# Cross attention with each quadrant's own maximum, a third projection bank and the first results moved

## The reference

```
q = x @ Wq + bq                  # 64 x 512, 16 heads of 32, scaled by 32**-0.5
k = ctx @ Wk + bk                # 1601 x 512
v = ctx @ Wv + bv                # 1601 x 512
s = q_h @ k_h.T, masked where the key is not valid      # 64 x 1601 for each head h
p = softmax(s)                   # over the 1601 keys
o = p @ v_h
```

## Time and profile before

| | us |
|---|---|
| median of three runs | 2890.74 (2889.43 to 2891.78) |
| the profiled execution, time | 2892.8 |
| the profiled execution, span from first to last instruction | 2891.1 |
| PE busy | 2660.4 |
| DVE busy | 1671.3 |
| ACT busy | 1441.8 |
| cross attention stage, about | 847 to 2318 |

### The profile page before, as it was taken

One profiled execution on the slowest core, in us unless ns is written; L12 is line 12 of the kernel. 1 busy time (PEld: TensorE's weight loads), 2 busy tenths in 40 slices (PEclk: granted clock), 3 DMA queues, 4 the chain that ended last, 5 costly groups with the idle time before them and its releaser, 6 DMA issues. The chain is left out here.

```text
span 2891.1 us, 58626 instructions
## 1 busy us (share of the span) xinstructions
PE 2660.4 (92%) x24696; PEld 2075.1 (72%) x24696; DVE 1671.3 (58%) x3485; ACT 1441.8 (50%) x2943; POOL 114.1 (4%) x104
## 2 busy tenths in 40 slices
PE   6999899899869999999999999999999987789987
PEld 3444677789757887778777877778777765667764
DVE  4333542557565555665655556655556678864487
ACT  2112222336435566565665656656666622725775
POOL 0000200120010000000000000000000013010000
PEclk9999999999979999999999999999999988899988
DMA  7998102347751011111111111111111020114300
GB/s 257 311 311 282 48 4 66 125 147 268 235 171 30 20 48 49 47 26 26 49 48 47 26 26 49 48 41 31 26 49 39 31 63 1 40 44 161 117 16 30
DMA packets 202932, 249.40 MB, mean 86 GB/s; under 512 B 77728, under 2 KB 132000, under 8 KB 202416
## 3 DMA queue, kind: packets, MB, share of 16 engines
q1 hardware_dynamic: 193456, 220.49, 24.2%
q10 hardware_dynamic: 6656, 16.78, 1.8%
q0 software_dynamic: 2560, 8.39, 0.8%
HBM read 221.50 MB, written 24.12 MB: 85 GB/s over the span
## 5 line engine op out<-in xcount | busy, mean ns | idle before, releaser
L91 PE MATMUL xa_J<-xa_c_hi,xa_wk_hi 128*128 128x402 f32 x1024 | 369.9, 361 | 1.7 <-POOL xa_m L2491 1.7
L2380 DVE TENSOR_TENSOR cl_v<-xa_J,main_x 128x512 f32<-128x512 f32 (+1 forms) x208 | 143.5, 690 | 390.2 <-PE xa_J L93 301.5
L93 PE MATMUL xa_J<-xa_c_hi,xa_wk_lo 128*128 128x402 f32 x1024 | 354.7, 346 | 0.0
L92 PE MATMUL xa_J<-xa_c_lo,xa_wk_hi 128*128 128x402 f32 x1024 | 354.5, 346 | 0.0
L2245 ACT ACTIVATE xa_kT<-xa_J,cl_bk 128x402 f32<-128x402 f32 x256 | 151.5, 592 | 383.7 <-PE xa_J L93 380.5
L91 PE MATMUL xa_J<-xa_wv_hi,xa_c_hi 128*128 128x512 f32 (+1 forms) x832 | 339.0, 407 | 0.4 <-ACT xa_kT L2245 0.4
L93 PE MATMUL xa_J<-xa_wv_hi,xa_c_lo 128*128 128x512 f32 (+1 forms) x832 | 327.7, 394 | 0.0
L92 PE MATMUL xa_J<-xa_wv_lo,xa_c_hi 128*128 128x512 f32 (+1 forms) x832 | 327.2, 393 | 0.0
L2258 ACT ACTIVATE xa_pr<-xa_pr,xa_nm 128x416 f32<-128x416 f32 x512 | 321.5, 631 | 3.9 <-DVE xa_nm L2364 3.9
L2264 ACT ACTIVATE xa_pr<-xa_pr,xa_ri 128x416 f32<-128x416 f32 x512 | 280.1, 630 | 60.4 <-DVE xa_ri L2368 60.1
L2354 DVE CUSTOM_DVE_ANT_0 xa_pr<-xa_S,xa_m 128x416 f32<-128x416 f32 x512 | 271.8, 587 | 43.6 <-PE xa_S L2536 29.3
(11 more groups left out here) (516 smaller groups left out, 4962.2 us busy)
## 6 DMA issues: line engine op xcount, KB each, us to landing
bl_rows<-in_ctx SPq DMA_DIRECT2D x40, 1024.0 KB, 8.8
main_x<-in_ctx_cols SPq DMA_DIRECT2D x192, 201.0 KB, 2.6
bl_cols<-in_ctx_cols SPq DMA_DIRECT2D x24, 1024.0 KB, 10.5
moe_raw<-in_L_ffn_routed_w SPq DMA_DIRECT2D x45, 512.0 KB, 4.8
main_qoT<-in_L_ffn_w ACTq DMA_DIRECT2D x32, 512.0 KB, 4.0
main_x<-in_ctx_cols SPq DMA_DIRECT2D x64, 197.5 KB, 3.3
main_qoT<-in_L_attn_W SPq DMA_DIRECT2D x16, 512.0 KB, 3.7
routed_in<-main_qoT SPq DMA_DIRECT2D x1, 7680.0 KB, 22.6
```

The source lines that it names most:

```text
L91: pe.matmul(out, w_hi, x_hi, start=first, stop=False)
L92: pe.matmul(out, w_hi, x_lo, start=False, stop=False)
L93: return pe.matmul(out, w_lo, x_hi, start=False, stop=last)
L2380: nc.vector.tensor_tensor(v[0:rows(n), value_slot(b, n), :], J[0:rows(n), place(b, ("v", n)) % 2, :], bv_sb[0:rows(n), :], ALU.add)\
```

## The change

Exponentials are taken with each partition's own maximum (that of its quadrant of the keys). `negate` turns the maxima into biases right behind the masks. When the exponentials are done, `weigh` copies biases and sums of the four quadrants beside each other on 32 partitions (four copies), takes the smallest bias and the differences to it; ACT takes their exponentials (`shares`); `invert` weighs the sums with the shares, adds them up, inverts, and writes share times inverse back to the four quadrants (four instructions) as `ri`, by which `normalise` scales as before.

PE loses `send_max`, `spread_max` and `sums`. The bank `E` goes to `J`, which now has three banks. `result(w)` at the end of a batch is moved behind the first key tile of the next batch, and the result after it behind the second key tile. ACT's copies of the key tiles and its exponentials are interleaved anew, and some of DVE's `turn`, `lows` and `keep_values` change places.

```diff
+BANKS = 3
...
+        local = s.sb("local", [P, 2, 2 * HG])
+        nm, rs = local[:, 0, :], local[:, 1, :]
+        parts = s.sb("parts", [QB, 4, 2, 2 * HG])
+        apart, share, weighed = (s.sb(n, [QB, 4, 2 * HG]) for n in ("apart", "share", "weighed"))
+        least, whole, inverse = (s.sb(n, [QB, 2 * HG]) for n in ("least", "whole", "inverse"))
...
-        J = s.ps("J", [P, 2, 512])
-        O, E = s.ps("O", [P, 512]), s.ps("E", [P, 512])
-        X, Y, Z = E[0:2 * HG, 0:P], E[:, P:P + 2 * HG], E[:, P + 2 * HG:P + 4 * HG]
+        J = s.ps("J", [P, BANKS, 512])
+        O = s.ps("O", [P, 512])
...
+                def shares(w):
+                    act.wait_ge(apart_ready, w + 1)
+                    nc.scalar.activation(share[:], apart[:], ACT.Exp).then_inc(share_ready, 1)
+
                 def normalise(w):
-                    act.wait_ge(inv_ready, w + 1)
+                    act.wait_ge(inv_ready, 4 * (w + 1))
...
                 def probabilities(w):
-                    exps(w - 1, 0, 4)
+                    keep_key(w, 0)
+                    exps(w - 1, 0, 3)
+                    keep_key(w, 1)
+                    exps(w - 1, 3, 6)
                     keep_key(w, 2)
-                    exps(w - 1, 4, 6)
+                    exps(w - 1, 6, 8)
                     keep_key(w, 3)
-                    exps(w - 1, 6, 8)
+                    shares(w - 1)
...
                 for b in range(BATCH):
                     w = GR * b
                     if b:
+                        keep_key(w, 0)
+                        exps(w - 1, 0, 2)
+                        keep_result(w - 4)
                         highs(b, 3, 0, 2)
-                        keep_result(w - 4)
-                        keep_key(w, 0)
+                        keep_key(w, 1)
                         highs(b, 3, 2, 4)
                         keep_result(w - 3)
-                        keep_key(w, 1)
-                        probabilities(w)
-                        keep_result(w - 2)
+                        exps(w - 1, 2, 5)
+                        keep_key(w, 2)
+                        exps(w - 1, 5, 8)
+                        keep_key(w, 3)
+                        shares(w - 1)
                         widen_mask(b)
                         normalise(w - 1)
-
-                    keep_key(w + 1, 0)
-                    keep_key(w + 1, 1)
+                        keep_result(w - 2)
+
                     probabilities(w + 1)
+                    normalise(w)
                     if b:
                         keep_result(w - 1)
-                    normalise(w)
-
-                    keep_key(w + 2, 0)
-                    keep_key(w + 2, 1)
+
                     probabilities(w + 2)
...
+                    if b == LAST:
+                        probabilities(w + 3)
+                        normalise(w + 2)
+                    else:
+                        keep_key(w + 3, 0)
+                        exps(w + 2, 0, 3)
+                        keep_key(w + 3, 1)
+                        exps(w + 2, 3, 6)
                         highs(b + 1, 0)
+                        keep_key(w + 3, 2)
+                        exps(w + 2, 6, 8)
+                        keep_key(w + 3, 3)
+                        shares(w + 2)
                         highs(b + 1, 1)
-                    probabilities(w + 3)
-                    normalise(w + 2)
-                    if b < LAST:
+                        normalise(w + 2)
                         highs(b + 1, 2)
...
-                def largest(w):
-                    dve.wait_ge(max_out, w + 1)
-                    nc.vector.tensor_reduce(gmax[:], X.rearrange("i (c q) -> i q c", c=4)[:, None, :, :].to_broadcast([2 * HG, 4, QB, 4]),
-                                            AX.X, ALU.max, negate=True).then_inc(gmax_ready, 1)
-
-                def keep_largest(w):
-                    dve.wait_ge(max_back, w + 1)
-                    nc.vector.tensor_copy(nm[:], Y).then_inc(nm_ready, 1)
-
-                def inverse(w):
-                    dve.wait_ge(summed, w + 1)
-                    nc.vector.reciprocal(ri[:], Z).then_inc(inv_ready, 1)
+                def negate(w):
+                    dve.wait_ge(masked, 2 * HG * (w + 1))
+                    nc.vector.tensor_scalar(nm, mx[:], -1.0, None, ALU.mult).then_inc(nm_ready, 1)
+
+                def weigh(w):
+                    dve.wait_ge(exp_done, 2 * HG * (w + 1))
+                    for c in range(4):
+                        nc.vector.tensor_copy(parts[:, c, :, :], local[QB * c:QB * (c + 1), :, :]).then_inc(gathered, 1)
+                    dve.wait_ge(gathered, 4 * (w + 1))
+                    nc.vector.tensor_reduce(least[:], parts[:, :, 0, :].rearrange("q c i -> q i c"), AX.X, ALU.min).then_inc(least_ready, 1)
+                    dve.wait_ge(least_ready, w + 1)
+                    nc.vector.tensor_tensor(apart[:], least[:, None, :].to_broadcast([QB, 4, 2 * HG]), parts[:, :, 0, :], ALU.subtract)\
+                        .then_inc(apart_ready, 1)
+
+                def invert(w):
+                    dve.wait_ge(share_ready, w + 1)
+                    nc.vector.tensor_tensor(weighed[:], share[:], parts[:, :, 1, :], ALU.mult).then_inc(weighed_ready, 1)
+                    dve.wait_ge(weighed_ready, w + 1)
+                    nc.vector.tensor_reduce(whole[:], weighed[:].rearrange("q c i -> q i c"), AX.X, ALU.add).then_inc(whole_ready, 1)
+                    dve.wait_ge(whole_ready, w + 1)
+                    nc.vector.reciprocal(inverse[:], whole[:]).then_inc(inverse_ready, 1)
+                    dve.wait_ge(inverse_ready, w + 1)
+                    for c in range(4):
+                        nc.vector.tensor_tensor(ri[QB * c:QB * (c + 1), :], share[:, c, :], inverse[:], ALU.mult).then_inc(inv_ready, 1)
...
                     if b:
-                        turn(w - 2, 0, 2)
-                        largest(w - 1)
-                        lows(b, 3, 0, 2)
-                        keep_largest(w - 1)
-                        lows(b, 3, 2, 4)
-                        turn(w - 2, 2, 8)
+                        turn(w - 2, 0, 3)
+                        lows(b, 3)
+                        turn(w - 2, 3, 8)
+                        weigh(w - 1)
                         keep_values(b, 0)
-                        inverse(w - 1)
+                        invert(w - 1)
                         masks(w, 0)
                         keep_values(b, 1)
                         masks(w, 1)
-
-                    largest(w)
+                        negate(w)
+
                     if b:
-                        turn(w - 1, 0, 2)
-                    keep_largest(w)
-                    if b:
-                        turn(w - 1, 2, 8)
+                        turn(w - 1, 0, 8)
+                        weigh(w)
+                        invert(w)
                         keep_values(b, 2)
                     else:
+                        weigh(w)
                         keep_values(b, 3)
-                    inverse(w)
+                        invert(w)
                     masks(w + 1, 0)
                     keep_values(b, 3 if b else 4)
                     masks(w + 1, 1)
+                    negate(w + 1)
                     if b and not last:
                         keep_values(b, 4)
...
+                    turn(w, 0, 8)
+                    weigh(w + 1)
                     keep_values(b, 4 if last else 5)
-                    inverse(w + 1)
+                    invert(w + 1)
...
                     else:
-                        turn(w + 1, 2, 5)
+                        turn(w + 1, 0, 8)
+                        keep_values(b, 9)
                         lows(b + 1, 0)
-                        keep_largest(w + 2)
-                        keep_values(b, 9)
-                        turn(w + 1, 5, 8)
+                        weigh(w + 2)
+                        keep_values(b, 10)
+                        invert(w + 2)
+                        masks(w + 3, 0)
                         lows(b + 1, 1)
-                        keep_values(b, 10)
-                        inverse(w + 2)
-                        masks(w + 3, 0)
                         keep_values(b, 11)
-                        lows(b + 1, 2, 0, 2)
                         masks(w + 3, 1)
+                        negate(w + 3)
                         keep_values(b, 12)
-                        lows(b + 1, 2, 2, 4)
+                        lows(b + 1, 2)
...
                 w = QUADS - 1
-                turn(w - 1, 0, 2)
-                largest(w)
+                turn(w - 1, 0, 4)
                 keep_values(LAST, 8)
-                turn(w - 1, 2, 4)
-                keep_largest(w)
+                turn(w - 1, 4, 8)
                 keep_values(LAST, 9)
-                turn(w - 1, 4, 8)
-                keep_values(LAST, 10)
                 for k in range(KC):
                     low_out(k)
+                weigh(w)
+                keep_values(LAST, 10)
```

(46 more changed lines are left out.)

34 lines of the change are left out of this document (10 added, 24 removed).

## The result

| | before | changed |
|---|---|---|
| median, us | 2890.09 (2888.26 to 2891.78) | 2838.07 (2836.60 to 2838.65) |
| profiled execution, us | 2892.8 | 2838.65 |
| its span, us | 2891.1 | 2836.9 |
| first key matmul of the stage to the first matmul of the next stage, us | 1474.81 | 1419.53 |
| of that: batch 0 | 86.13 | 83.97 |

Four executions of each kernel stand beside one another; the ratio is 0.9819, with a 95% interval of 0.9802 to 0.9836. The gain is 52 us by the medians and 54 by the profiled executions, where 68 was forecast: 2838.07 against 2822.7, and 1 us outside of the range. The stage gave 55.3, of which the 15 full batches gave 53.8 against 65.6 forecast, batch 0 gave 2.2 against 1.8, and the tail lost 0.7 where it was to gain 0.6. What lies behind the stage takes 569.1 us before and 568.4 after.

What follows compares the result with a forecast made beforehand. PE was taken to bound the stage: 4.37 us a batch over 15 batches (65.6), 1.8 in batch 0 and 0.6 in the tail made 68 us, so a median of 2822.7 us, with an 8 in 10 range of 2815 to 2837.

Steps and rivals of the forecast that it cites:

- batch 0: The first batch, without a first quad or results: three quads at 0.60 us each, a gain of 1.8 us.
- the tail: The end of the stage: one set of small matmuls goes, a gain of 0.6 us.
- What bounds the kernel: PE ends the cross attention stage; work taken off it gains its whole distance, work added to DVE or ACT is free.
- The moved result: At a batch's end: PE's trip over DVE's copy of value tile 12 goes, gaining 1.75 us a batch, and 0.1 more.
- The small matmuls: On PE: removing the two transposes and their pauses gains 0.49 us per quad without results; removing sums gains 0.11 or 0.32.
- The third bank: PE's projection banks: the added bank gains nothing by itself, only covering later copies on ACT and DVE.
- The length of `invert`: On DVE ahead of the masks: 0.9 us if four operations overlap, 1.4 if all seven are chained; 1.2 taken.
- the due time of the fourth mask: In a tight quad, needed 4.6 us after the first scores start, so `invert` may last 1.65 us without cost.
- rival B: `invert` takes 2.0 us, costing 0.35 in each of 33 tight quads, 12 us: 2834 us; chance 0.12.
- A: Pauses around PE's small matmuls belong to waits and banks and stay; only 55 us gained, 2836 us; chance 0.09.
- C: DVE's small operations cost 0.68 us each like the replaced reduction, `invert` 4.8: 2949 us, slower by 58; chance 0.03.
- D: Batch 0's exponentials start earlier and an early PE pause goes, 2 to 5 us more, 2819 us; chance 0.15.

Runs made afterwards that it cites:

- e1: The changed kernel with `invert` ahead of the value copy in the five places where it stood behind one; 2827.78 us, ratio to before 0.9779.
- e7: The changed kernel without the exchange between quadrants, each partition normalised by its own sum; 2822.04 us, ratio to before 0.9762.
- e4: The changed kernel with the first result of a batch back at the batch's end; 2865.63 us, ratio to before 0.9911.
- e5: The kernel before with only its first two results moved behind the next batch's first and second key tiles, ACT's copies with them; 2864.79 us.
- e6: The changed kernel with two banks and, in 48 quads, two transposes of constants where the old ones stood; 2862.22 us, ratio to before 0.9898.
- e3: The changed kernel with two projection banks instead of three; 2838.93 us, ratio to before 0.9820.
- e2: The changed kernel with the reciprocal in `invert` taken twice, the second waiting for the first; 2846.85 us, ratio to before 0.9851.
- e2b: e1 with the reciprocal in `invert` taken three times in a chain; 2831.12 us, ratio to before 0.9787.
- e10: The changed kernel run once more, unaltered; 2836.82 us, ratio to before 0.9810.
- e8: e1 with, in the tail, the copy of value tile 12 ahead of the turns and `weigh` and `invert` ahead of the low parts; 2831.46 us.
- e9: e8 with value tile 3 put between the first two halves of the scores in batch 0; 2824.26 us, ratio to before 0.9766.
- e11: e9 with DVE's low parts ahead of `weigh` again in the tail; 2824.47 us, ratio to before 0.9758.

## Why the prediction was wrong in size

**What bounds the kernel: right.** PE did. Removing its waits and small matmuls gave nearly their whole distance, and 768 more instructions on DVE gave nothing away in the full batches where they lay beside PE's work (e1 against e7).

**The moved result: right.** 1.85 a batch forecast, 1.63 (e4) and 1.83 (e5) measured. No wait for `c_lo` or for `turned` took its place.

**The small matmuls: right.** 8.91 us for four key tiles (8.9 forecast); e6 shows that 0.45 for a pair of transposes, where 0.49 was forecast, is the price of the matmuls themselves. The third bank was given nothing and is worth nothing (e3).

**The length of `invert`: right, at the upper end.** 0.9 to 1.4 was given, 1.2 taken, 1.41 measured. The three chained steps start 0.20 to 0.23 after one another, and the four products take 0.72 for four, 0.18 each and not the 0.08 of an overlapped one. By the Trainium skill, VectorE: DVE Perf Modes, section "Two Vector instructions with no wait between them", they had to, since they write to four quadrants; the trace agrees. Taking the rule's 1.4 would by itself not have changed the sum, since the step below allowed 1.65. With the due time right it would have counted: by the estimate of 1.06, an `invert` of 1.2 costs (1.2 - 1.06) x 33 = 4.6 us and one of 1.41 the 11.5 measured.

**The failed step: the due time of the fourth mask.** The prediction says "its fourth head, three quarters of 0.9 later, needs the fourth mask at t + 4.6. In hundredths, I may be 1.65 us." I had divided the half's 0.91 us equally among its four heads, as if they ran one after another. They don't. All 32 weight loads of a half pass in 0.23 us, the four heads run beside one another, and the 0.91 is common to them. Taken one by one, the 32 matmuls of a free half start in two groups of 16, at 1413.66 to 1413.76 and at 1414.03 to 1414.13, so the fourth head's first matmul starts within 0.1 us of the first head's. Worked back from the measured loss, the fourth mask is due at about t + 4.0 and `invert` may last about 1.06. It lasted 0.35 more, in 33 quads: 11.5 us, 10.4 of them in the 15 batches. That is the size and the wait of rival B (0.35 in 33 quads, 12 us, 2834), which I gave 0.12; it came by another road, for `invert` was not 2.0 long but the margin was 0.6 shorter. e1 takes the 10.3 us out, e2 adds 0.23 to each as such a due time demands, and e2b shows twice that addition nearly free elsewhere (0.5 us in the 15 batches).

**The rest.** Without that term (e1) the 15 batches give 64.2 us where 65.6 was forecast. The transposes are 1.9 of what is missing (20.2 by e6 for 22.1). That batch 0 gave 2.2 (1.8 in e10) for the 1.8 forecast is partly luck: three late masks, about 1.0, are in it, and its stretch at the 1.2 GHz level differs between executions. Without the late masks (e1) it is 2.8. The tail was put at +0.6 and came at -0.7 (-0.35 in e10). The forecast counted only its small matmuls there; I had not followed DVE's list in the tail, where the copy of value tile 12 now stands behind four turns that wait for ACT's later scaling, so that PE waits 2.0 us for it and not 0.8. e8 removes that wait.

**Rivals.** A falls by e6, B's place is shown with another cause, C falls by the 0.20 us reductions. D, the early pause of PE, did not come by itself; it is there to be had (e9).

## What to carry to other kernels

When a chain is moved off the bound engine, its length matters less than where it stands: the same seven instructions cost 10 us between a copy and the masks and nothing ahead of the copy. Read due times from the first use, here the weight loads, and never from an equal share of a group's duration, since packed matmuls start together. Follow the moved order through the first batch and the tail as well; they hold their own waits. Here they gave 7 us more of the stage (e1 to e11), though the medians' ratios, 0.9779 and 0.9758, hardly tell the two apart.

## What the runs showed of the hardware

- Four heads packed in the array as 32 x 32 tiles load all 32 weights in 0.23 us and are done after 0.91 us together; a fourth head whose weights are 0.22 us late makes the whole group 0.35 later on average.
- A pair of tiny transposes between tiles of 12 matmuls costs PE 0.45 us even when nothing waits (e6), more than their own distances of 0.02 and 0.16; the tile behind each starts slower (2.37 and 2.31 against 2.17 and 2.20).
- After PE's wait for the first masks the granted clock fell in batch 0 of the changed kernel (0.70 over 872 to 879 us), and it fell in every other kernel here that has this wait but one, e7. In e9, where a value tile fills the wait, it stayed (1.00). It also fell in e1's tail, after PE had waited 2.34 us for the last value copy, and 104 matmuls took 3.00 us instead of 1.66. The window of e7's batch 0, then that of e1's tail:

```profile
867.00:874.00 7.00, 7.00 (x42) 7.00 (x39) 1.32 (x7) 4.45 (x10) 0.00 (x0) 1.00 0.01 2
```

```profile
2239.30:2242.30 3.00, 2.97 (x104) 2.73 (x104) 1.91 (x4) 0.83 (x2) 0.00 (x0) 0.50 0.55 164
```

  0.50 is the 1.2 GHz level. The changed kernel waited 2.00 us at the same place and stayed at 1.00, while in e4 it fell after 1.99 (0.63 over 2279.4 to 2282.2 us). What decides stays open.
- PE paused for 3.9 us with nothing to wait for while 195 GB/s of other transfers ran (e8), and for 2.2 in two pauses when the reload came earlier (e11). A 0.02 MB load of instructions landed 1.28 us ahead of the end of e8's pause, and 1.39 and 1.31 us ahead of the ends of e11's.
